# Three loads reordered on the DMA queue of an attention stage, and key_max moved ahead of one x_lo

## The reference

```python
x = x + xattn(layernorm(x), ctx, Wq, bq, Wk, bk)   # x, ctx: (8, 256, 1024)
x = x + ffn(layernorm(x), gate, up, down)          # hidden size 3584, NF4 codes

def xattn(text, features, Wq, bq, Wk, bk):
    Q = text @ Wq.T + bq
    K = features @ Wk.T + bk
    attn = softmax(Q @ K.T / sqrt(1024))
    return attn @ features
```

## Time and profile before

| | us |
|---|---|
| median of 3 runs | 1962.15 |
| lowest and highest | 1959.35 and 1962.42 |
| the profiled execution | 1962.42 |
| its span in the trace | 1960.6 |
| PE busy | 1911.0 (97%) |
| DVE busy | 1631.9 (83%) |
| ACT busy | 1452.6 (74%) |
| POOL busy | 385.0 (20%) |

### The profile page before, as it was taken

One profiled execution on the slowest core, in us unless ns is written; L12 is line 12 of the kernel. 1 busy time (PEld: TensorE's weight loads), 2 busy tenths in 40 slices (PEclk: granted clock), 3 DMA queues, 4 the chain that ended last, 5 costly groups with the idle time before them and its releaser, 6 DMA issues.

```text
span 1960.6 us, 29547 instructions
## 1 busy us (share of the span) xinstructions
PE 1911.0 (97%) x9744; PEld 968.3 (49%) x9744; DVE 1631.9 (83%) x2742; ACT 1452.6 (74%) x2710; POOL 385.0 (20%) x584
## 2 busy tenths in 40 slices
PE   8989999889999999999999999999999999989999
PEld 3468788644444444444444444444444444434444
DVE  6768899877898898898898898898798898876963
ACT  3767767557989889989988988988999999800000
POOL 0012534430121111121121111121133222201010
PEclk9999999999999999999999999999999999999999
DMA  9123999973645545555455555456478998993462
GB/s 348 31 72 91 217 291 261 228 278 86 146 135 113 140 135 123 136 139 125 124 147 126 121 145 128 121 141 134 118 209 227 247 230 206 234 238 127 163 226 86
DMA packets 427417, 323.00 MB, mean 165 GB/s; under 512 B 361088, under 2 KB 361088, under 8 KB 425344
## 3 DMA queue, kind: packets, MB, share of 16 engines
q1 hardware_dynamic: 381152, 167.47, 38.1%
q0 software_dynamic: 44032, 153.65, 24.1%
q10 hardware_dynamic: 2080, 0.01, 0.1%
HBM read 154.31 MB, written 82.31 MB: 121 GB/s over the span
## 4 chain that ended last, share of the span: by engine, by line
PE 55%; ACT 21%; DVE 8%; issue 6%; POOL 2%; DMA 2%; SPq 0%; DVEq 0%; ACTq 0%; POOLq 0%
PE ps L2097 38%; PE ps L2139 11%; ACT sq L346 7%; ACT sq L342 5%; PE ps L1522 3%; ACT w L346 2%; POOL T L1429 2%; ACT w L342 2%; DVE w L362 1%; ACT halves L414 1%; DMA T<-halves 1%; DVE tail L2249 1%; ACT tail L2170 1%; DVE T L1735 1%; PE ps L1554 1%
## 5 line engine op out<-in xcount | busy, mean ns | idle before, releaser
L2097 PE MATMUL ps<-T,wS 128*128 128x512 f16 x4704 | 1017.6, 379 | 4.1 <-DVE ps L2204 2.5
L2097 PEld LDWEIGHTS ps<-T,wS 128*128 128x128 f16 x4704 | 459.8, 98 | 558.4 <-issue 4.8
L346 ACT ACTIVATE sq<-sq 128x512 f32<-128x512 f32 x898 | 516.5, 628 | 0.0
L362 DVE SCALAR_TENSOR_TENSOR w<-sq,w 128x512 f32<-128x512 f32 x590 | 418.6, 709 | 113.0 <-ACT sq L346 103.2
L342 ACT ACTIVATE sq<-q 128x512 f32<-128x512 int32 x598 | 363.3, 633 | 49.4 <-DVE w L362 47.7
L2139 PE MATMUL ps<-T,tail 128*128 128x512 f16 x1584 | 346.6, 380 | 8.2 <-DMA T<-halves 3.3
L2139 PEld LDWEIGHTS ps<-T,tail 128*128 128x128 f16 x1584 | 154.9, 98 | 197.5 <-issue 7.3
L2139 PE MATMUL ps<-T,wS 128*128 128x512 f16 x768 | 168.5, 379 | 3.6 <-DMA T<-halves 3.4
L1522 PE MATMUL ps<-T 128*128 128x256 f16 x1536 | 170.2, 273 | 1.9 <-DVE T L1735 1.9
L430 DVE SCALAR_TENSOR_TENSOR halves<-w,halves 128x512 f16<-128x512 f32 x240 | 162.8, 688 | 7.7 <-ACT halves L414 7.4
L2045 POOL DMA_DIRECT2D keep_h<-tail x196 | 106.3, 542 | 295.9 <-DVE tail L2249 293.6
(11 more groups left out here) (221 smaller groups left out, 1813.7 us busy)
## 6 DMA issues: line engine op xcount, KB each, us to landing
keep_h<-tail POOLq DMA_DIRECT2D x196, 256.0 KB, 2.6
tail<-keep_h POOLq DMA_DIRECT2D x66, 512.0 KB, 4.9
wS<-keep_h POOLq DMA_DIRECT2D x32, 512.0 KB, 5.3
q<-in_L_ffn_down_q POOLq DMA_DIRECT2D x56, 256.0 KB, 4.3
q<-in_L_ffn_up_q POOLq DMA_DIRECT2D x52, 256.0 KB, 3.0
q<-in_L_ffn_gate_q POOLq DMA_DIRECT2D x48, 256.0 KB, 3.4
keep_x<-T SPq DMA_DIRECT2D x38, 256.0 KB, 4.4
T<-in_x SPq DMA_DIRECT2D x9, 1024.0 KB, 7.9
```

Source lines behind the costliest of these rows:

```text
L346: nc.scalar.activation(place, place, ACT.Square, bias=b, scale=a).then_inc(un.s_act, 1)
L362: nc.vector.scalar_tensor_tensor(out=out, in0=square_place(un, u, i - 1), scalar=FACTORS[i - 1][1], in1=un.w[:, buf, :], op0=ALU.add, op1= ...
L2097: last = nc.tensor.matmul(ps[:, bank, :], un.wS[:, z % SLOTS, a, kt, :], t.Tp[side][product][:, :, b, kt, :], start=fresh and n == 0, stop ...
```

## The change

On SP, in the steps of the attention, three loads change places. The x_feed load goes from behind the first t_next to ahead of turn_keys. The y_rows load goes from behind the second t_next to right behind turn_keys. The keys load goes from right behind turn_keys to behind the first t_next, ahead of the second. The waits in front of each load go with it. On DVE, key_max(b+1) changes places with x_lo(b+1, 3).

```diff
             if b >= 3:
                 t_next(c - 1, 5)
                 t_next(c - 1, 6)
-            units_due(base + 1, base + 2, base + 3, base + 4)
+            units_due(base + 1, base + 2)
+            if b >= 2 and b + 2 < BATCH:
+
+                sp.wait_ge(s_xn, TB * b if b == 2 else TB * (b + 1))
+                sp.dma_start(x_feed(b + 2), t.x_t[:, TB * (b + 2):TB * (b + 3), :]).then_inc(s_xf, 16)
+            units_due(base + 3, base + 4)
             turn_keys(b, 0)
             turn_keys(b, 1)
-            if b < LAST:
-
-                sp.wait_ge(s_klo, TB * (b + 1))
-                sp.dma_start(keys[:, :, :], t.ctx_t[b + 1]).then_inc(s_keys, 16)
-            units_due(base + 5, base + 6)
-            if b >= 2:
-                t_next(c, 0)
-            if b >= 2 and b + 2 < BATCH:
-
-                sp.wait_ge(s_xn, TB * b if b == 2 else TB * (b + 1))
-                sp.dma_start(x_feed(b + 2), t.x_t[:, TB * (b + 2):TB * (b + 3), :]).then_inc(s_xf, 16)
-            units_due(base + 7)
-            if b >= 2:
-                t_next(c, 1)
             if b >= 2:
 
                 if more:
@@
                 sp.dma_start(y_rows(t, b)[:, :, :], t.x_t[:, TB * b:TB * (b + 1), :]).then_inc(s_xr[b % TB], 16)
+            units_due(base + 5, base + 6)
+            if b >= 2:
+                t_next(c, 0)
+            units_due(base + 7)
+            if b < LAST:
+
+                sp.wait_ge(s_klo, TB * (b + 1))
+                sp.dma_start(keys[:, :, :], t.ctx_t[b + 1]).then_inc(s_keys, 16)
+            if b >= 2:
+                t_next(c, 1)
             units_due(base + 8)
@@
             if more:
                 x_lo(b + 1, 2)
+                key_max(b + 1)
                 x_lo(b + 1, 3)
-                key_max(b + 1)
```

More of the change, by code:

```diff
@@ L1371, in step @@
                 t_next(c - 1, 6)
-            units_due(base + 1, base + 2, base + 3, base + 4)
-            turn_keys(b, 0)
-            turn_keys(b, 1)
-            if b < LAST:
-                sp.wait_ge(s_klo, TB * (b + 1))
-                sp.dma_start(keys[:, :, :], t.ctx_t[b + 1]).then_inc(s_keys, 16)
-            units_due(base + 5, base + 6)
-            if b >= 2:
-                t_next(c, 0)
+            units_due(base + 1, base + 2)
             if b >= 2 and b + 2 < BATCH:
@@ L1385, in step @@
                 sp.dma_start(x_feed(b + 2), t.x_t[:, TB * (b + 2):TB * (b + 3), :]).then_inc(s_xf, 16)
-            units_due(base + 7)
-            if b >= 2:
-                t_next(c, 1)
+            units_due(base + 3, base + 4)
+            turn_keys(b, 0)
+            turn_keys(b, 1)
             if b >= 2:
```

## The result

| | before | changed |
|---|---|---|
| median, us | 1959.35 (9 runs) | 1971.35 (9 runs) |
| lowest and highest | 1950.91 and 1962.42 | 1966.37 and 1975.83 |
| span of the profiled execution | 1960.6 | 1975.4 |

These are runs side by side on one chip. The ratio of the changed kernel to the one before is 1.0075, with a 95% interval of 1.0058 to 1.0092: 0.75% slower, which is 14.7 us of 1962; the two medians of the table differ by 12.0. The forecast was 6.9 us. The direction was right; the size was too small by a factor of about two. That 1971.35 us lies inside the forecast's range (1961.5 to 1974.0) is in part luck: the range was wide, and the forecast counted from 1962.15 us, the median of three runs, where the nine of this table have 1959.35. Counted from 1962.15, 0.75% more is 1976.9 us, which is outside.

What follows compares the result with a forecast made beforehand. It took the attention cycle from key_max to key_max as bound, with PE, DVE and DMA near full. Delay of 0.7 + 7.0 = 7.7 us, less 0.8, gave 6.9: 1969.3, adjusted to 1969.1 us, range 1961.5 to 1974.

Steps and rivals of the forecast that it cites:

- x_feed earlier, cost 0: On SP ahead of turn_keys: the megabyte fits idle DMA time or delays only key transposes not needed until the scores; 0.
- rival four: Early x_feed delays key transposes, or keys land at 10 us and more; about 1974 to 1976 us; chance 0.07.
- y_rows earlier, cost 0 by itself, fills the place: On SP behind turn_keys: its waits are already met and nobody needs it early; 0, but takes the keys load's place.
- The keys load 2.6 us later and 8.4 us to landing: On SP: keys issued 2.6 us later, landing in 8.4 instead of 6.3; the 3.7 us cover ahead of key_max is gone.
- key_max ahead of x_lo 3: On DVE: x_lo 3 ends 2.9 us after key_max starts (K), delaying R; keys_lo moves 0.65 us further from K.
- The sum: Attention cycle, key_max to key_max: 37.1 us against 35.4, 1.75 a step, 7.0 us over four steps.
- The end: Step 7: PE's late_lo wait shrinks from 3.64 to 1.6 us; PE goes on 7.7 us late, less 0.8 gained.
- The y_rows gain of 0.8 us: Step 7: earlier y_rows lands the last transpose sooner, cutting PE's 1.70 us t_sum wait; 0 to 1.7, taken as 0.8.
- The marks: Trace signs of being right: PE waits 2 to 4 us at R, key_max waits for keys, period 36.5 to 37.5 us.
- Two: Rival: keys still land in time, under 6.8 us, so key_max comes 0.65 us earlier a step; 1958 us; chance 0.10.
- three: Rival: landing of 7.5 us just meets today's key_max, period stays 35.4, step 7's slack absorbs R's delay; 1962; chance 0.12.
- The estimate of 4.4 us for a megabyte: Skill's DMA rule, 2.0 us plus bytes over 436 GB/s: keys would land at 282.0 and key_max never wait.

Runs made afterwards that it cites:

- number 6: Kernel before with only x_feed moved ahead of turn_keys; 1964.44 us, ratio 1.0010.
- number 4: Changed kernel with x_feed put behind the second t_next; 1970.41 us, ratio 1.0048 to the kernel before.
- number 10: Changed kernel with y_rows back in third place, so no megabyte goes out just ahead of the late keys load; 1967.62 us, ratio 1.0031 to the kernel before.
- number 7: Changed kernel with the reciprocal root chain, scales(c), moved ahead of the two t_lo on DVE; 1983.34 us, ratio 1.0114 to the kernel before.
- 8: Kernel before with key_max ahead of x_lo 3 and the reciprocal root chain ahead of the two t_lo, DMA order unchanged; 1961.42 us, ratio 0.9994.
- number 9: Changed kernel with one Newton round fewer in the second normalisation's reciprocal root; 1971.62 us, ratio 1.0044 to the kernel before.
- Number 2: Changed kernel with key_max back behind x_lo 3, so only SP's order differs from the kernel before; 1972.63 us, ratio 1.0051 to the latter.
- number 1: Kernel before with only key_max moved ahead of x_lo 3 on DVE, SP's order unchanged; 1958.38 us, ratio 0.9980.
- 5: Changed kernel with keys and y_rows exchanged, keys load right behind turn_keys again; 1960.56 us, ratio 0.9985 to the kernel before.
- number 3: Changed kernel with 14 idle PE matmuls ahead of R from step 4 on; 1975.51 us, ratio 1.0070 to the kernel before.

## Why the prediction was right in direction and wrong in size

- *x_feed earlier, cost 0.* On its own not settled by the time (number 6: 1.0010, an interval that holds both nothing and 4 us), and in its trace one step of four became 3 us longer. In the new order it is wrong by about 1 us a step (number 4), since the time in which the delay was absorbed is gone. This is a part of rival four, which was given 0.07 as a whole and excluded from the sum.
- *y_rows earlier, cost 0 by itself, fills the place.* Right as a mechanism, and its price is now measured: 1.9 us of landing for the keys and 1 us of issue (number 10). The prediction held it inside the 8.4.
- *The keys load 2.6 us later and 8.4 us to landing.* Nearly right: 3.23 and 8.80. The cover of 3.7 us was gone, key_max waited in each of five steps, though in step 2 only 0.45 us and with no delay against before (213.69 for 214.00; 214.7 foretold).
- *key_max ahead of x_lo 3, "keys_lo moves 0.65 us further from K".* **This is the step that failed.** The term was 0.65 us and it measured 1.85 (21.52 less 19.67). The prediction moved DVE's later work by one x_lo and left its length, and POOL's place beside it, as they were. The small operations of the reciprocal root came to lie in POOL's work. Numbers 7 and 8 take the meeting away with the same operations and number 9 with 0.8 us of operations less: keys_lo comes back to 20.1 (in number 7 in three steps of four) and 19.55. Number 2, which has no shift, has no stretch (19.51). The exchange alone (number 1) brings 0.98 of the 1.85 us, with a meeting in two steps of four; in the changed kernel they meet in all four, since POOL's first low half stood 16.3 us behind key_max in the mean, not 16.7. What makes POOL sooner there, no run isolates. For what holds the two engines apart, the Trainium skill bears on this: the page "GPSIMD Engine Reference", section "Specifications", says that POOL's SBUF interfaces are shared with VectorE, with contention for DVE instructions that read two SBUF inputs or run in a two-port mode. The trace agrees for the operations with two inputs (L233 0.16 to 0.69 us, L1165 0.16 to 0.58); x_lo, whose one input is in PSUM, stayed at 0.66 to 0.69 us beside POOL and without it. L234 has a single tensor input and was stretched too (0.17 to 0.61), and no run here tells in which mode it ran.
- *The sum.* (37.1 less 35.4) x 4 was 7.0 us. It measured (39.75 less 35.39) x 4 = 17.4. The excess of 2.65 us a step is 1.4 for the term above, 0.6 and 0.4 for the second place with y_rows in front, 0.3 for the turns of the keys. Part of these is the early x_feed, since putting it behind the second t_next (number 4) took 0.3 off the turns and 0.6 off the landing. All four errors have one sign, and I read it so, though no run isolates it: each figure came from a step that still had slack around it, and a cycle without slack pays for every delay.
- *The end.* R of step 7 started 2.94 us behind key_max, as said; the wait at the second late_turn shrank by 2.7 us, from 3.64 to 0.96, where 2.0 was said. The y_rows gain of 0.8 us was tied to a wait of PE that did vanish (1.70 to none), but it vanished in numbers 5, 6 and 10 too, where y_rows goes out late: the reason given is not borne out.
- *The marks.* Right: the waits of R behind x_lo in steps 3 to 7 (0.9 to 5.0 us for 2 to 4), key_max's waits for the load, keys landing 7.7 to 9.5 us after issue, no wait of PE for t_sum. Off: the period (36.5 to 37.5 foretold), R of step 7 at 375.61 for 366 and y_rows of step 7 at 397.2 for 386, all three by about the same excess; of the waits at turn_x number 2 two stayed, 4.3 us in all, and of those at turn_probs one, 1.2 us.
- *The rivals.* Two (the keys land in time) and three (hidden again) are refuted by the 16.3 us of key_max's waits. Four had the right order of time, 1974 to 1976, with a reason, the early x_feed, that explains 1.15 of the 2.65 us a step. The estimate of 4.4 us for a megabyte, set against these, uses a fit that the Trainium skill, page "DMA: Bandwidth & Descriptors", section "Anatomy of one DMA", gives for DMAs issued by GpSimd. The loads here are issued by SP, and they landed in 6.3 and 8.5 us by the median.

The clock of PE was in none of the terms. It fell, and it cost nothing (number 3).

## What to carry to other kernels

When an instruction is moved on one engine, look at what the whole rest of that engine's chain then lies beside, on the engine that shares its memory interfaces above all: tiny operations with a fixed length are the ones that grow three- or fourfold. When a wait is added to a cycle that had slack, do not sum medians of the slack state; take the slow end of each link, since none of them is forgiven any more (this reading is argued above, not shown by a run). And if a DMA is moved to a later place, what counts is what stands just ahead of it: here one megabyte in front cost 1.9 us of landing and 1 us of issue.

## What was not expected of the hardware

- DVE operations on 128x2 elements (f32) took 0.16 to 0.27 us where no tensor_tensor of POOL ran beside them, 1409 of them in the thirteen profiles from 130 to 470 us. Of the 78 that lay wholly beside one, 76 took 0.52 to 1.31 us, 0.60 by the median.
- The effect goes both ways: POOL's 128x1 subtraction took 0.57 us with a decoding operation of DVE (L430 in step 4) beside it and 0.19 to 0.20 with an x_lo.
- In the changed kernel, where PE had stood for 2.5 to 5.0 us ahead of R, the granted clock over the first 48 matmuls was 0.69 to 0.76 (7.1 to 7.7 us, not 5.41). After stops of 0.4 to 2.1 us with fillers ahead of them (number 3) it was 1.00. Without fillers, in number 10, a stop of 2.04 us was followed by 0.76 and one of 1.95 by 1.00.
- The keys load of 1 MB landed in 6.2 to 6.6 us by the median of a profile with no other megabyte just ahead of it, and in 7.6 to 8.5 us behind y_rows.
